# A four-block graph network on one Trainium2 core: the edge weights move to the narrow operand of the matrix-building matmuls, and ScalarE clears every second reused PSUM block

## The chip, the cores and the metric

The kernel runs on one core of one Trainium2 chip. The metric is the device time of one execution in microseconds; lower is better. The core's engines are TensorE (PE in the profile; its weight loads are PEld), VectorE (DVE), ScalarE (ACT), GpSimd (POOL) and SyncE (SP).

## The reference

512 nodes with 512 features each, and 16384 edges sorted by their destination, go through four graph blocks. Each takes `h = relu(layernorm(x))` and adds its result to `x`. Cut to what matters here:

```python
edge_index = stack([src, dst])
x = x + L0(h)   # adj[src,dst] = adj[dst,src] = 1, + I; row-normalised; h@W, then 3 hops of adj @ cur
x = x + L1(h)   # sum_r segment_sum((h[src] @ W_rel[r] + b_rel[r]) * weight * (type == r), dst), / degree; FFN, two layer norms
x = x + L2(h)   # adj[src,dst] = 1, + I, d^-1/2 adj d^-1/2 @ (h @ W)
x = x + L3(h)   # two SAGE layers: mean of h[src] over dst, @ Wl.T, + x @ Wr.T
```

So five 512x512 matrices are wanted from the edge list: for each of the four edge types r the sum of the weights of the edges src to dst, and the count of edges src to dst, from which the unweighted adjacencies come. The function `build_matrices` makes them; `run_blocks` does everything else.

## The kernel before

**The work around the change.** The 16384 edges are 128 chunks of 128 edges, in order of destination; an edge of a chunk sits on a partition. For a chunk PE multiplies one-hot rows: the stationary operand says which of 128 values the low part of `src` has, the moving operand says which destination, edge type and high part of `src` (4 of them) the edge has. The edges of one chunk reach only few destinations, so the moving operand has `WIDE` = 8 destinations from a base on, which is the first destination of the chunk rounded down to an even number (`base`, L321). The columns are then NT x R x WIDE = 4 x 4 x 8 = 128 for the weights and 4 x 8 = 32 for the counts. A float32 weight is split in `V` = 3 bfloat16 parts, and before the change the parts stand in the stationary operand: `wgt_hot` is the low one-hot `lo_hot` times a part. So a chunk is three matmuls of 128 columns (L585) and one of 32 columns (L587), into PSUM at a register offset.

**The PSUM blocks.** Sixteen destinations (`DB`) make a block of 4 x 5 x 22 = 440 float32 columns in one PSUM bank: 16 destinations and 6 of overhang (`TAIL`). There are 32 blocks in 8 banks. PE clears a block with a matmul of zeros of 440 columns (`zero`, L577) before its first chunk, `opens(b)` = 4b - 7. After the last chunk of a block, `closes(b)` = 4b + 7, ACT copies its 16 destinations to `wall` (L279) and its overhang to `tails` (L281), in `keep_block`. DVE adds the overhangs in later (`add_tails`, L416).

**Groups.** 16 chunks (`G`) are a group; there are 8, called group 0 to 7 here. DVE builds the one-hots of a group in a ring of `RING` = 3: `low_hot` and the two `key_hots` by comparison (L370), then the weighted ones by `weigh` (L376). From group 3 on, ACT makes half of the third part (`weigh_some`, L273, 8 instructions a group). DVE waits for PE to have finished the group three before. PE waits for the hots of a group, and reads the 16 PSUM offsets of a group into registers with one TENSOR_LOAD (L550), those of groups 0 to 2 during the projection, of the others ahead of the group. Each matmul at a register offset has an instruction in front that makes its address (printed as ISA). Group 7 is made in two halves, FRONT and BACK.

**Before and behind.** Ahead of the chunks PE runs matmuls of zeros (`spin`), transposes and the projection `h @ W` (L561). Behind them DVE has a fixed list: three `add_tails`, the copy of the early counts (L420), splits and products for block L0 (L434, L426, L429), one more `add_tails`, two splits, then it waits for all chunks, copies the last block (L466), adds its overhang, and signals `built`. With that the copy of the last counts (L515) releases PE (L654) and SyncE's weight loads for the later blocks. Then `run_blocks` begins with the hops (L1132). The order on each engine is written out by hand; semaphores are the only link. A flag computed on the chip (`slow_flag`, L336 to L349) sends all engines down another, much longer path where a chunk's destinations don't fit `WIDE`.

## Time and profile before

| what | value |
|---|---|
| median of 3 runs | 386.3 us (385.6 to 386.51) |
| the profiled execution's own time | 386.04 us |
| its span | 384.1 us, 4220 instructions |
| PE busy | 368.6 us, 96% |
| DVE busy | 181.6 us, 47% |
| ACT busy | 91.5 us, 24% |
| mean granted TensorE clock | 0.991 |

The span is from the first to the last instruction; 1.9 us of the execution's own time lie outside it. Busy shares are averages over stages with different limits. The stretch in which the chunks run is 29 to 69 us of the span, a tenth of it.

### The profile page before, as it was taken

What the parts mean: (1) busy time and instruction counts of PE and PEld (TensorE: products, weight loads), DVE (VectorE), ACT (ScalarE), POOL (GpSimd) and SP (SyncE); (2) the same over time, 40 slices, a digit from 0 to 9 for tenths busy, and PEclk for the clock granted to TensorE, in tenths of its full rate; (3) what the DMA queues carried; (4) which work ended last, traced back from release to release, by engine and by line L of the source; (5) the groups of instructions that cost most, each with busy time, mean ns of one, the idle gap of its engine ahead of it and who ended that gap; (6) DMA issues with size and microseconds to landing.
All of it is one profiled execution on the core that took longest, in us unless ns stands there. A gap on an engine that the chain in (4) does not pass through costs nothing.

```text
span 384.1 us, 4220 instructions
## 1 busy us (share of the span) xinstructions
PE 368.6 (96%) x1554; PEld 205.7 (54%) x1554; DVE 181.6 (47%) x329; ACT 91.5 (24%) x213; POOL 57.9 (15%) x48
## 2 busy tenths in 40 slices
PE   6999787899999999999999999999999999999996
PEld 2448676788444444444444447544455757445642
DVE  5898999968832122236320332004685447212311
ACT  3446986132510000000000102321124270212000
POOL 5000000000589700010001001000211064000000
PEclk9899999899999999999999999999999999999999
DMA  7000000399000000029100018027333000000011
GB/s 249 25 2 2 3 2 2 140 295 363 25 2 0 0 0 0 0 100 355 65 0 0 2 30 189 0 42 124 56 53 59 0 0 2 0 0 0 2 55 55
DMA packets 43812, 22.05 MB, mean 57 GB/s; under 512 B 35536, under 2 KB 36048, under 8 KB 43792
## 3 DMA queue, kind: packets, MB, share of 16 engines
q1 hardware_dynamic: 43264, 20.85, 19.8%
q0 software_dynamic: 240, 0.79, 0.7%
q8 instruction: 14, 0.23, 0.2%
q10 hardware_dynamic: 288, 0.13, 0.1%
q14 instruction: 6, 0.05, 0.0%
HBM read 20.72 MB, written 1.05 MB: 57 GB/s over the span
## 4 chain that ended last, share of the span: by engine, by line
PE 84%; DVE 12%; DMA 1%; ACT 1%; issue 1%; ACTq 0%; DVEq 0%
PE bank L1132 46%; PE bank L1206 14%; PE bank L1325 7%; PE bank L1237 7%; DVE slots L376 4%; PE bank L561 4%; DVE slots L370 3%; PE bank L1120 2%; PE bank L522 1%; DVE wall L416 1%; DMA bias<-in_edge_type 1%; PE bank L585 1%; DVE lo L434 1%; DVE stats L945 1%; PE bank L1148 0%
## 5 line engine op out<-in xcount | busy, mean ns | idle before, releaser
L1132 PE MATMUL bank<-slots,h_t 128*128 128x512 f32 x192 | 83.6, 592 | 0.8 <-ACT h_t L868 0.8
L1132 PEld LDWEIGHTS bank<-slots,h_t 128*128 128x128 f32 x192 | 35.9, 190 | 43.6 <-issue 43.6
L1206 PE MATMUL bank<-slots,wall 128*128 128x512 f32 x128 | 55.7, 593 | 0.0
L1206 PEld LDWEIGHTS bank<-slots,wall 128*128 128x128 f32 x128 | 24.0, 190 | 28.7 <-issue 28.7
L585 PE MATMUL bank<-slots 128*128 128x128 bf16 x384 | 31.8, 219 | 5.7 <-DVE slots L370 3.3
L1013 DVE TENSOR_TENSOR slots<-bank,bias 128x512 f32<-128x512 f32 x16 | 11.1, 692 | 43.9 <-PE bank L1132 43.9
L585 PEld LDWEIGHTS bank<-slots 128*128 128x128 bf16 x384 | 25.0, 97 | 9.0 <-issue 6.5
L1132 PE MATMUL bank<-wall,h_t 128*128 128x512 f32 x64 | 29.0, 594 | 0.5 <-ACT h_t L868 0.5
L1325 PE MATMUL bank<-wall,slots 128*128 128x512 f32 x64 | 28.4, 592 | 0.0
L1132 PE MATMUL bank<-h_t,slots 128*128 128x384 f32 (+2 forms) x96 | 28.0, 451 | 0.0
L1237 PE MATMUL bank<-slots 128*128 128x512 f32 x64 | 27.8, 592 | 0.0
L1132 PE MATMUL bank<-hi,adj 128*128 128x512 f32 x64 | 26.6, 415 | 0.0
L1132 PE MATMUL bank<-lo,adj 128*128 128x512 f32 x64 | 25.8, 403 | 0.0
L376 DVE TENSOR_TENSOR slots<-slots,inv_cnt 128x2048 bf16<-128x2048 bf16 (+1 forms) x26 | 25.5, 1030 | 0.0
L857 ACT ACTIVATE columns<-mean_var,eps 128x1 f32<-128x1 f32 x20 | 5.9, 293 | 74.7 <-DVE mean_var L946 74.6
L370 DVE TENSOR_TENSOR slots<-inv_cnt,both_ways 128x2048 bf16<-128x2048 f16 (+3 forms) x27 | 21.9, 860 | 2.2 <-PE bank L587 1.7
L587 PE MATMUL bank<-slots 128*128 128x32 bf16 x128 | 22.7, 178 | 0.0
L1132 PEld LDWEIGHTS bank<-h_t,slots 128*128 128x128 f32 x96 | 15.7, 191 | 11.6 <-issue 7.7
L1237 PEld LDWEIGHTS bank<-slots 128*128 128x128 f32 x64 | 12.1, 190 | 14.8 <-issue 14.8
L1325 PEld LDWEIGHTS bank<-wall,slots 128*128 128x128 f32 x64 | 12.1, 190 | 14.5 <-issue 14.4
L1030 DVE SCALAR_TENSOR_TENSOR h<-bank,columns,h 128x512 f32<-128x512 f32 x4 | 3.0, 751 | 35.4 <-PE bank L1206 35.4
L818 POOL TENSOR_TENSOR h<-h,bias 128x512 f32<-128x512 f32 x4 | 5.1, 1266 | 95.3 <-PE bank L1120 95.3
(163 smaller groups left out, 452.3 us busy)
## 6 DMA issues: line engine op xcount, KB each, us to landing
slots<-in_L_gnn_W_rel SPq DMA_DIRECT2D x4, 1024.0 KB, 11.1
slots<-in_L_gnn_W_ffn SPq DMA_DIRECT2D x2, 2048.0 KB, 12.8
slots<-in_L_gnn_Wl SPq DMA_DIRECT2D x32, 64.0 KB, 2.4
slots<-in_L_gnn_Wr SPq DMA_DIRECT2D x32, 64.0 KB, 2.4
x<-in_x SPq DMA_DIRECT2D x4, 256.0 KB, 5.4
bias<-in_L_gnn_W SPq DMA_DIRECT2D x1, 1024.0 KB, 7.4
slots<-in_L_gnn_W_self SPq DMA_DIRECT2D x1, 1024.0 KB, 5.8
bias<-in_L_gnn_b_rel SPq DMA_DIRECT2D x4, 256.0 KB, 10.2
```

The source lines that it names most:

```text
L370: return dve.tensor_tensor(to[:, pairs], have, want, ALU.is_equal)
L376: dve.tensor_tensor(wgt_hot[:, s, v, pairs], lo_hot[:, s, pairs], by, ALU.mult).then_inc(hots_ready, 1)
L561: ins = pe.matmul(proj_bank[m], h_t[:, k, m * P:(m + 1) * P], w0[:, k, :], start=(k == 0), stop=(k == KT - 1))
L585: pe.matmul(place[:, :, 0:R, 0:WIDE], wgt_hot[:, s, v, a, :, j], key_hot[:, s, a, :, j], start=False, stop=False, skip_group_check=True)
L587: pe.matmul(place[:, :, R, 0:WIDE], lo_hot[:, s, a, :, j], cnt_hot[:, s, a, :, j], start=False, stop=False, skip_group_check=True).then_in ...
L857: act.activation(std[:, t:t + 1], mean_var[:, t, 1:2], ACT.Sqrt, bias=eps[:]).then_inc(std_ready[n], 1)
L1013: dve.tensor_tensor(msg[r][:, m, :], main[m][:], brel[r], ALU.add).then_inc(msg_out, 1)
L1120: ins = pe.transpose(t_bank[use % 2][:, i * P:(i + 1) * P], b, ident[:])
L1132: ins = pe.matmul(bank, left, right, start=start and i == 0, stop=stop and i == len(pairs) - 1)
L1206: ins = pe.matmul(main[m][:], wall[:, r, s, tile(m)], msg[r][:, s, :], start=(r == 0 and s == 0), stop=(r == R - 1 and s == NT - 1))
L1237: ins = pe.matmul(main[m][:], hid[:, g, tile(m)], wf2[:, g, :], start=(g == 0), stop=(g == GT - 1))
L1325: ins = pe.matmul(sage_bank[m][:], agg_t[layer][:, k, tile(m)], sage(wl, k), start=False, stop=(k == KT - 1))
```

## The change

`WIDE` is 7, and the base is the first destination of the chunk, odd or even. `lo_hot` alone is the stationary operand of every matmul of a chunk. The weights move to the other side: a table `typ_hot` (chunk, type) is made once, times the three parts of the weight (`typ_wgt`, 512 elements a part), and `weigh` multiplies the count one-hots `cnt_hot` (4 x 7 = 28 columns) by it. The weighted hots of part 0 and the count hots are neighbours in `cnt_wgt_hot`, so a chunk is one matmul of 5 x 28 = 140 columns and two of 4 x 28 = 112. ACT makes no hots any more. For every second block from 9 on (9, 11, ... 31) ACT writes the zeros (L285 of the changed kernel), and PE waits for that in place of its own matmul of zeros. The overhang stays 6 and a block 440 columns.

```diff
-WIDE = 8
+WIDE = 7
...
-TAIL = DB - 2 + WIDE - DB
+TAIL = DB - 1 + WIDE - DB
...
-BY_ACT = 8
-ACT_FROM = 3
...
-assert N == D and E % P == 0 and CH == P and NT * R * WIDE == P and NT * OUT_R * COLS <= 512
+assert N == D and E % P == 0 and CH == P and NT * R * WIDE <= P and NT * OUT_R * COLS <= 512
...
-        lo_hot, key_hot = in_slots(BF16, RING, G // 2, P, 2), in_slots(BF16, RING, G // 2, P, 2)
-        cnt_hot, wgt_hot = in_slots(BF16, RING, G // 2, NT * WIDE, 2), in_slots(BF16, RING, V, G // 2, P, 2)
+        lo_hot, cnt_wgt_hot = in_slots(BF16, RING, G // 2, P, 2), in_slots(BF16, RING, G // 2, OUT_R, NT * WIDE, 2)
+        cnt_hot, wgt_hot = cnt_wgt_hot[:, :, :, R], in_slots(BF16, RING, V - 1, G // 2, R, NT * WIDE, 2)
+        typ_hot, typ_wgt = in_slots(BF16, CH // 2, R, 2), in_slots(BF16, V, CH // 2, R, 2)
...
-        lo_set, hots_ready, chunk_done = sem("lo_set"), sem("hots_ready"), sem("chunk_done")
-        block_out = sem("block_out")
+        cnt_set, hots_ready, chunk_done = sem("cnt_set"), sem("hots_ready"), sem("chunk_done")
+        block_out, act_zeroed = sem("block_out"), sem("act_zeroed")
...
+        def zeroed_by_act(b):
+            return b >= 9 and b < NB and b % 2 == 1
...
-            def weigh_some(g):
-                act.wait_ge(lo_set, g + 1)
-                for c in range(BY_ACT):
-                    act.activation(wgt_hot[:, g % RING, V - 1, c // 2, :, c % 2], lo_hot[:, g % RING, c // 2, :, c % 2], ACT.Copy,
-                                   scale=rest[:, 1, g * G + c:g * G + c + 1]).then_inc(act_hots_ready, 1)
...
-                act.wait_ge(parts_ready, 1)
-                kept = 0
-                for g in range(1, CH // G + 1):
-                    if ACT_FROM <= g < CH // G:
-                        weigh_some(g)
-                    while kept < NB - 1 and closes(kept) < g * G:
-                        keep_block(kept)
-                        kept += 1
+                for b in range(NB - 1):
+                    keep_block(b)
+                    if b > 0 and zeroed_by_act(b + 7):
+                        act.wait_ge(block_out, 2 * b)
+                        act.activation(psum[(b + 7) % 8][:, 0:NT * OUT_R * COLS], zeros[:, 0:NT * OUT_R * COLS], ACT.Copy)\
+                            .then_inc(act_zeroed, 1)
...
-            lo, key, cnt_key, apart = (e_f32[:, i, :] for i in range(4))
-            base, bank_of, col_of = (base_i[:, i:i + 1] for i in range(3))
+            lo, cnt_key, kind, apart = (e_f32[:, i, :] for i in range(4))
+            base, bank_of, col_of = e_int[:, 0, 0:1], base_i[:, 1:2], base_i[:, 2:3]
...
-            link(dve.tensor_scalar(base, e_int[:, 0, 0:1], N - 2, None, ALU.bitwise_and))
...
-                 dve.tensor_scalar(col_of, base, DB - 2, None, ALU.bitwise_and),
+                 dve.tensor_scalar(col_of, base, DB - 1, None, ALU.bitwise_and),
...
-            link(dve.scalar_tensor_tensor(key, typ, float(WIDE), apart, ALU.mult, ALU.add))
-            dve.scalar_tensor_tensor(key, high_i, float(R * WIDE) / P, key, ALU.mult, ALU.add).then_inc(keys_ready, 1)
+            dve.tensor_copy(kind, typ).then_inc(keys_ready, 1)
...
-                s = g % RING
-                by = chunks(parts[:, v, :], g, pairs).unsqueeze(2).broadcast_to([P, pairs.stop - pairs.start, P, 2])
-                dve.tensor_tensor(wgt_hot[:, s, v, pairs], lo_hot[:, s, pairs], by, ALU.mult).then_inc(hots_ready, 1)
+                s, count = g % RING, pairs.stop - pairs.start
+                to = cnt_wgt_hot[:, s, pairs, 0:R] if v == 0 else wgt_hot[:, s, v - 1, pairs]
+                at = slice(g * G // 2 + pairs.start, g * G // 2 + pairs.stop)
+                dve.tensor_tensor(to, cnt_hot[:, s, pairs].unsqueeze(2).broadcast_to([P, count, R, NT * WIDE, 2]),
+                                  typ_wgt[:, v, at].unsqueeze(3).broadcast_to([P, count, R, NT * WIDE, 2]),
+                                  ALU.mult).then_inc(hots_ready, 1)
...
-                hot(lo_hot[:, g % RING], 0, g, pairs, P).then_inc(lo_set, 1)
-            def key_hots(g, pairs):
-                hot(key_hot[:, g % RING], 1, g, pairs, P).then_inc(hots_ready, 1)
-                hot(cnt_hot[:, g % RING], 2, g, pairs, NT * WIDE).then_inc(hots_ready, 1)
+                hot(lo_hot[:, g % RING], 0, g, pairs, P).then_inc(hots_ready, 1)
+            def count_hot(g, pairs):
+                hot(cnt_hot[:, g % RING], 1, g, pairs, NT * WIDE).then_inc(cnt_set, 1)
...
+                count_hot(g, WHOLE)
...
-                key_hots(g, WHOLE)
-                dve.wait_ge(lo_set, g + 1)
-                for v in range(V - 1):
+                dve.wait_ge(cnt_set, g + 1)
+                for v in range(V):
...
-                weigh(g, V - 1, BACK if g >= ACT_FROM else WHOLE)
...
+                count_hot(g, FRONT)
+                count_hot(g, BACK)
...
-                key_hots(g, FRONT)
+                dve.wait_ge(cnt_set, g + 2)
+                for v in range(V):
+                    weigh(g, v, FRONT)
...
-                dve.wait_ge(lo_set, g + 1)
-                for v in range(V - 1):
-                    weigh(g, v, FRONT)
-                key_hots(g, BACK)
-                dve.wait_ge(lo_set, g + 2)
...
-                low_hot(0, WHOLE)
+                types = chunks(keys_t[:, 2, :], 0, slice(0, CH // 2)).unsqueeze(2).broadcast_to([P, CH // 2, R, 2])
+                kinds = pair_iota[:, 0:R, :].unsqueeze(1).broadcast_to([P, CH // 2, R, 2])
+                dve.tensor_tensor(typ_hot, types, kinds, ALU.is_equal).then_inc(typ_set, 1)
+                count_hot(0, WHOLE)
...
-                key_hots(0, WHOLE)
+                dve.wait_ge(typ_set, 1)
+                for v in range(V):
+                    by = chunks(parts[:, v, :], 0, slice(0, CH // 2)).unsqueeze(2).broadcast_to([P, CH // 2, R, 2])
+                    dve.tensor_tensor(typ_wgt[:, v], typ_hot, by, ALU.mult).then_inc(typ_set, 1)
...
-                dve.wait_ge(lo_set, 1)
-                weigh(0, 0, WHOLE)
+                low_hot(0, WHOLE)
...
-                for v in range(1, V):
+                dve.wait_ge(cnt_set, 1)
+                dve.wait_ge(typ_set, 1 + V)
+                for v in range(V):
...
+                if zeroed_by_act(b):
+                    pe.wait_ge(act_zeroed, (b - 7) // 2)
+                    return
                 if b >= 8:
...
-                for v in range(V):
-                    pe.matmul(place[:, :, 0:R, 0:WIDE], wgt_hot[:, s, v, a, :, j], key_hot[:, s, a, :, j],
-                              start=False, stop=False, skip_group_check=True)
-                pe.matmul(place[:, :, R, 0:WIDE], lo_hot[:, s, a, :, j], cnt_hot[:, s, a, :, j],
-                          start=False, stop=False, skip_group_check=True).then_inc(chunk_done, 1)
+                low = lo_hot[:, s, a, :, j]
+                pe.matmul(place[:, :, :, 0:WIDE].rearrange("p h r d -> p r h d"), low, cnt_wgt_hot[:, s, a, :, :, j],
+                          start=False, stop=False, skip_group_check=True)
+                for v in range(V - 1):
+                    ins = pe.matmul(place[:, :, 0:R, 0:WIDE].rearrange("p h r d -> p r h d"), low, wgt_hot[:, s, v, a, :, :, j],
+                                    start=False, stop=False, skip_group_check=True)
+                ins.then_inc(chunk_done, 1)
...
-                            pe.wait_ge(hots_ready, (V + 2) * (g + 1) - (0 if g < CH // G - 1 else 1))
-                            if g >= ACT_FROM:
-                                pe.wait_ge(act_hots_ready, BY_ACT * (g - ACT_FROM + 1))
-                        elif c == CH - G + BY_ACT:
-                            pe.wait_ge(hots_ready, (V + 2) * (g + 1) + V + 1)
+                            pe.wait_ge(hots_ready, (V + 1) * (g + 1))
+                        elif c == CH - G // 2:
+                            pe.wait_ge(hots_ready, (V + 1) * (g + 2))
```

On PE, the rows of group 3 from its load of offsets on; `slots` are the one-hots, `both_ways` the zeros. Before:

```order
L550 TENSOR_LOAD both_ways
L585 ISA
L585 MATMUL bank<-slots 128x4x4x8 x3
L587 ISA
L587 MATMUL bank<-slots 128x4x8
L577 MATMUL bank<-both_ways 128x440
L585 ISA
L585 MATMUL bank<-slots 128x4x4x8 x3
L587 ISA
L587 MATMUL bank<-slots 128x4x8
L585 ISA
```

And of the changed kernel:

```order
L549 TENSOR_LOAD both_ways
L587 ISA
L587 MATMUL bank<-slots 128x5x4x7
L590 MATMUL bank<-slots 128x4x4x7 x2
L579 MATMUL bank<-both_ways 128x440
L587 ISA
L587 MATMUL bank<-slots 128x5x4x7
L590 MATMUL bank<-slots 128x4x4x7 x2
L587 ISA
L587 MATMUL bank<-slots 128x5x4x7
L590 MATMUL bank<-slots 128x4x4x7 x2
L587 ISA
```

A chunk has three matmuls for four and one address instruction for two; its runs in PSUM are 7 columns long for 8.

On DVE, the rows of group 4, from its wait for PE on; L370 compares, L376 multiplies, L416 adds overhangs. Before:

```order
L370 TENSOR_TENSOR slots<-inv_cnt,both_ways 128x2048 [waits chunk_done]
L370 TENSOR_TENSOR slots<-inv_cnt,both_ways 128x2048
L370 TENSOR_TENSOR slots<-inv_cnt,both_ways 128x512
L376 TENSOR_TENSOR slots<-slots,inv_cnt 128x2048 [waits lo_set]
L376 TENSOR_TENSOR slots<-slots,inv_cnt 128x2048
L376 TENSOR_TENSOR slots<-slots,inv_cnt 128x1024
L416 TENSOR_TENSOR wall<-wall,bias 128x20x4x6 [waits block_out]
```

And of the changed kernel (L362 compares, L369 multiplies, L408 adds overhangs):

```order
L362 TENSOR_TENSOR slots<-inv_cnt,both_ways 128x8x56 [waits chunk_done]
L362 TENSOR_TENSOR slots<-inv_cnt,both_ways 128x2048
L369 TENSOR_TENSOR slots<-slots 128x8x224 [waits cnt_set]
L369 TENSOR_TENSOR slots<-slots 128x1792 x2
L408 TENSOR_TENSOR wall<-wall,bias 128x20x4x6 [waits block_out]
L362 TENSOR_TENSOR slots<-inv_cnt,both_ways 128x8x56 [waits chunk_done]
```

A group has one comparison of 2048, one of 448 and three products of 1792 elements, for two of 2048, one of 512, and products of 2048, 2048 and 1024; nothing of it is left to ACT.

On ACT, rows in the middle of the chunks; `wall` and `bias` receive a kept block. Before:

```order
L281 ACTIVATE bias<-bank 128x4x5x6
L273 ACTIVATE slots<-slots 128x128 [waits lo_set]
L273 ACTIVATE slots<-slots 128x128 x7
L279 ACTIVATE wall<-bank 128x4x5x16 [waits chunk_done]
L281 ACTIVATE bias<-bank 128x4x5x6
L279 ACTIVATE wall<-bank 128x4x5x16 [waits chunk_done]
L281 ACTIVATE bias<-bank 128x4x5x6
```

And of the changed kernel:

```order
L275 ACTIVATE wall<-bank 128x4x5x16 [waits chunk_done]
L277 ACTIVATE bias<-bank 128x4x5x6
L285 ACTIVATE bank<-both_ways 128x440 [waits block_out]
L275 ACTIVATE wall<-bank 128x4x5x16 [waits chunk_done]
L277 ACTIVATE bias<-bank 128x4x5x6
L275 ACTIVATE wall<-bank 128x4x5x16 [waits chunk_done]
L277 ACTIVATE bias<-bank 128x4x5x6
L285 ACTIVATE bank<-both_ways 128x440 [waits block_out]
```

The eight scaled copies of a group are gone, and behind every second kept block stands a write of 440 zeros to the bank that was kept one block earlier.

## Rows read from the trace of the kernel before

**Rows 1.** Page of the profile, part 4: shares of the chain by line

```profile
...
PE bank L1132 46%; PE bank L1206 14%; PE bank L1325 7%; PE bank L1237 7%; DVE slots L376 4%; PE bank L561 4%; DVE slots L370 3%; PE bank L1120 2%; PE bank L522 1%; DVE wall L416 1%; DMA bias<-in_edge_type 1%; PE bank L585 1%; DVE lo L434 1%
...
```

**Rows 2.** Chain that ended last, in order: start us, us, engine, output, line

```profile
...
5.01 0.29 DVE bias L332
...
33.49 2.70 DVE slots L370 x3
...
39.05 2.60 DVE slots L370 x3
41.66 2.87 DVE slots L376 x3
...
57.20 2.01 DVE slots L370 x4
...
63.02 1.72 DVE wall L416 x3
...
70.73 0.41 DVE wall L466
...
72.28 0.55 PE bank L654 x3
...
```

**Rows 3.** Groups from 29 to 73 us, shapes apart: busy us, mean ns

```profile
...
L585 PE MATMUL bank<-slots 128*128 128x128 bf16 x384 | 31.8, 219 | 5.7 <-DVE slots L370 3.3 <-ACT slots L273 1.2 <-issue 1.2
...
L587 PE MATMUL bank<-slots 128*128 128x32 bf16 x128 | 22.7, 178 | 0.0
L279 ACT ACTIVATE wall<-bank 128x320 f32<-128x320 f32 x31 | 13.6, 440 | 9.6 <-PE bank L587 9.5
L376 DVE TENSOR_TENSOR slots<-slots,inv_cnt 128x2048 bf16<-128x2048 bf16 x11 | 12.9, 1216 | 0.0
...
L281 ACT ACTIVATE bias<-bank 128x120 f32<-128x120 f32 x31 | 8.5, 275 | 0.0
L376 DVE TENSOR_TENSOR slots<-slots,inv_cnt 128x1024 bf16<-128x1024 bf16 x9 | 5.9, 681 | 0.0
...
L370 DVE TENSOR_TENSOR slots<-inv_cnt,both_ways 128x512 bf16<-128x512 f16 x4 | 1.7, 416 | 0.0
...
```

**Rows 4.** Timeline of PE: start us, us, line, operation, count

```profile
...
33.68 0.34 PE L585 MATMUL bank<-slots 128*128 128x128 bf16 x3
...
33.88 0.33 PE L585 MATMUL bank<-slots 128*128 128x128 bf16 x3
...
34.48 0.35 PE L577 MATMUL bank<-both_ways 128*128 128x440 bf16 x1
34.66 0.34 PE L585 MATMUL bank<-slots 128*128 128x128 bf16 x3
...
41.11 0.18 PE L587 MATMUL bank<-slots 128*128 128x32 bf16 x1
42.27 0.35 PE L585 MATMUL bank<-slots 128*128 128x128 bf16 x3 [0.98 <-DVE slots L370]
...
67.50 0.34 PE L585 MATMUL bank<-slots 128*128 128x128 bf16 x3
...
67.75 0.34 PE L585 MATMUL bank<-slots 128*128 128x128 bf16 x3
...
68.49 0.18 PE L587 MATMUL bank<-slots 128*128 128x32 bf16 x1
...
```

**Rows 5.** Offset loads of L550 on PE's queue: duration ns min/median/max

```profile
...
L550 PEldq TENSOR_LOAD <-both_ways x8: 1102/1105/1292, 13.7 to 62.9; - x8
...
```

**Rows 6.** Windows: us, busy by engine, PEclk (granted clock), DMA, GB/s

```profile
...
69.00:74.00 5.00, 3.76 (x25) 3.48 (x25) 4.44 (x11) 0.31 (x2) 0.00 (x0) 0.94 0.14 49
74.00:78.00 4.00, 4.00 (x13) 3.22 (x12) 3.43 (x11) 0.00 (x0) 0.00 (x0) 0.65 1.03 372
...
```

**Rows 7.** Timeline of ACT with a backlog

```profile
...
40.23 0.42 ACT L279 ACTIVATE wall<-bank 128x320 f32<-128x320 f32 x1
...
40.70 0.44 ACT L279 ACTIVATE wall<-bank 128x320 f32<-128x320 f32 x1
...
```

More of the change, by code:

```diff
@@ L162, in build_matrices @@
         const_set, ident_ready, const_ready = sem("const_set"), sem("ident_ready"), sem("const_ready")
-        zeros_set, act_hots_ready = sem("zeros_set"), sem("act_hots_ready")
+        zeros_set, typ_set = sem("zeros_set"), sem("typ_set")
         eye_set, iota_ready = sem("eye_set"), sem("iota_ready")
@@ L179, in build_matrices @@
         chunked = "(c e) -> c e"
-        WHOLE, FRONT, BACK = slice(0, G // 2), slice(0, BY_ACT // 2), slice(BY_ACT // 2, G // 2)
+        WHOLE, FRONT, BACK = slice(0, G // 2), slice(0, G // 4), slice(G // 4, G // 2)
         most = slice(0, N - P)
@@ L550, in offsets @@
                 return nc.values_load_multi_w_load_instructions(
-                    off_row[0:1, g * G:(g + 1) * G], [PE], min_val=0, max_val=7 * N + DB - 2,
+                    off_row[0:1, g * G:(g + 1) * G], [PE], min_val=0, max_val=7 * N + DB - 1,
                     skip_runtime_bounds_check_because="masked to that on the chip")[1]
```

## The prediction

> **What bounds the kernel now.** I read the shares of the chain first: nearly all of the span is PE in the blocks behind the matrices (the hops, L1132, and L1206, L1237, L1325), which the change doesn't touch [rows 1]. In the stretch of the chunks the chain lies on DVE. It enters DVE at 33.49, when PE has finished group 0 and a place in the ring is free, and stays there: group 4 is 2.60 of comparisons (39.05) and 2.87 of products (41.66), group 7 begins at 57.20, the hots are done at 63.02, the fixed list behind them runs to the copy of the last block at 70.73, and PE takes over at 72.28 [rows 2]. So hots made faster pull everything behind them forward, until something else is later than the list.
>
> PE is that something, and close. In group 1 a chunk follows the last one after 0.20 (33.68, 33.88), and a matmul of zeros takes 0.18 (34.48, 34.66). Groups 0 to 2 end at 41.11, and the next chunk starts only at 42.27; the last chunk ends at about 68.6 [rows 4]. The gap is no lack of hots: group 3's were done at 39.05 [rows 2]. It is the TENSOR_LOAD of the offsets, 1.1 us each time [rows 5], which starts when the queue is empty. So PE's groups 3 to 7 take (68.49 - 41.11) / 5 = 5.48 each [rows 4]: 16 x 0.196 + 4 x 0.19 = 3.9 of matmuls (0.196 is the pitch of chunks to three digits) and 1.58 around the load. DVE needs all chunks at 70.73, so PE has 2.1 us in hand.
>
> **DVE, part by part.** Instructions overlap by 0.08: two comparisons of 2048 and one of 512 have means of 1216 (the product's mean, the form costs the same) and 416, in sum 2.85, and take 2.60 [rows 2, 3]. The slope is (1216 - 681) / 1024 = 0.52 ns an element [rows 3]. Then 1792 elements take 1.00 net, 448 take 0.30, 2048 take 1.14, 1024 take 0.60, 896 take 0.53 and 224 take 0.19. A group after: 0.30 + 1.14 + 3 x 1.00 = 4.45, for 2.60 + 2.87 = 5.47 before. That is 1.02 less in each of groups 3 to 6: 4.1. Group 7 took 63.02 - 57.20 = 5.82 and will take 2 x 0.19 + 2 x 0.60 + 6 x 0.53 = 4.77: 1.05. The `add_tails` between groups stay as they are.
>
> I take the new products at the same slope. They read both inputs with a step of 0 in some dimension, but innermost are pairs of neighbouring 16-bit values as before. If they fell to one element per step, 0.52 ns more for each of 1792 elements, a group would take 2.8 more. The other end is no cost below the slope: nothing in the rows runs faster.
>
> The first three groups and the table (four instructions of 512, 0.33 each, 1.3 in sum) lie ahead of 33.49, where DVE waited 1.66 for PE; they cost nothing, since the shorter groups 0 to 2 also give back more than that. If PE came earlier, this cover would still hold by some 4 us.
>
> **The start.** DVE enters the chain by group 0 of PE. Two things bring that forward. Ahead of the transposes one copy stands for two products of 0.29 (L331, L332) [rows 2]; that is up to 0.33, and 0.15 if the fixed zeros matmuls behind it swallow half; I take 0.2. And PE's group 0 is shorter. A column at 2.4 GHz is 0.42 ns, and the 440 columns of zeros take that, 0.18 [rows 4]. A chunk before has 3 x 128 + 32 = 416 columns, 0.173, and takes 0.196: 0.006 over for each of four matmuls. A chunk after has 140 + 2 x 112 = 364 columns, 0.152, and three times 0.006: 0.170. Group 0 is 16 x 0.026 = 0.4 shorter. Together 0.6.
>
> Sum: 4.1 + 1.05 + 0.6 = 5.75, call it 5.8.
>
> **Does PE stay ahead?** It starts at 29.2. Groups 0 to 2: 48 chunks and 9 zeros (blocks 2 to 8, 10, 12; the others are ACT's). Groups 3 to 7: 80 chunks, 9 zeros, five loads at 1.58. With c for a chunk, PE ends at 29.2 + 18 x 0.19 + 7.9 + 128c = 40.5 + 128c. For c = 0.170 that is 62.3, and DVE asks at 70.7 - 5.8 = 64.9: 2.6 us of room. It is filled at c = 0.191. The whole gain is gone at c = (70.7 - 40.5) / 128 = 0.236. Where PE's sequencer sets the pace, with no zeros in between, chunks came every 0.25 (67.50, 67.75) [rows 4]; with one address instruction and three matmuls for two and four this is 0.125 (by the address instructions) to 0.19 (by the matmuls), and I take it as no slower than the array. If it stayed 0.25 in groups 3 to 7, a group would take 16 x 0.25 + 1.58 = 5.6, PE would end near 67, and some 2 of the 5.8 would go.
>
> **ACT.** It loses eight copies a group and gains two writes of 440 zeros. L279 and L281 give (440 - 275) / 200 = 0.83 ns a column, so 440 columns take 0.54 [rows 3]. With a backlog a kept block takes 0.47 (40.23, 40.70) [rows 7]. A group is then 4 x 0.47 + 2 x 0.54 = 3.0 for 4.45 of DVE: idle. In groups 0 to 2 eight chunks take PE 8 x 0.170 + 0.19 = 1.55 and ACT 2 x 0.47 + 0.54 = 1.48: just enough, with 14 chunks between the block kept before the write and the chunk that needs it. Behind the waiting PE instruction all chunks are queued; a lag of ACT would cost PE at most the 0.54 each time, from its 2.6 of room.
>
> **The branch.** The 128 chunks of the reference's inputs reach at most 5 destinations beyond their first, and 7 allow 6, so the long path isn't taken.
>
> **The hops.** At 73 to 77 the granted clock fell to the lower of its two levels (0.94 and 0.65 in the two windows, 3.4 us at 1.2 GHz in sum), right behind PE's pause before L654; it cost 1.7 [rows 6]. After the change PE is done with the chunks at 62.3, turns the early counts, and then has nothing until 72.3 - 5.8 = 66.5: a longer pause, so a low stretch at the hops is at least as likely. It may be as long (0), longer, at most double (+1.7), or fall where PE is idle (-1.7). I take 0 and keep both ends. A low clock among the chunks, where PE's matmuls would fill 3.1 of the 5.0 us of a DVE group for 3.9 of 5.5, I hold unlikely: the gap of a load was 1.16 [rows 4] and grows no longer.
>
> **Forecast.** 386.04 - 5.8 = 380.2 for the profiled execution, whose own time is 0.3 below the median of the runs; so 380.5 as the median. Its own range is 378 to 382.
>
> **Rivals.** *PSUM runs of odd length.* The new columns lie in runs of 7 from any column on; before, runs of 8 from an even one. No row of before shows such a write. For it: the base was rounded down to an even number at the price of an eighth column, and contiguous zeros and runs of 8 have the same 0.42 ns a column, so runs that start even are the only thing known to be fast. Against it: nothing shown. The lower bound is no cost, c = 0.170. If a run of 7 costs as one of 8, a chunk is 160 + 2 x 128 = 416 columns again, 0.191: PE ends at 64.9, just in time. If columns are written in pairs of the stream, and pairs that straddle two even places go twice, two runs of 7 take 11 steps for 7: 364 x 11 / 7 = 572 columns, c = 0.256, PE ends at 73.3, the list waits from 70.7 on, 2.6 slower: 389. If every column takes double, c = 0.31, PE ends at 80.2, 9.5 slower: 396. This decides from c = 0.236 on. The Trainium skill, PSUM — Partial Sum Buffer, section Specifications (TRN2), has 8-byte lines (two float32) and says that any access that is not contiguous slows matmuls significantly. For runs of 8 the trace disagrees, whose chunk takes 0.196 for 416 columns; by its rule applied to the new runs the time would be the 389 to 396 just given. The rival has 0.14.
>
> *PE takes over in part.* c between 0.19 and 0.23, by the writes or the sequencer, or zeros that come late from ACT: 381 to 385.5, at 383. 0.15.
>
> *Nothing gained.* c near 0.236, or the DVE gain eaten by a second low stretch and a late PE together: 386. 0.05.
>
> *DVE's products lose the pairs, or the clock falls among the chunks.* Five groups x 2.8 - 5.8 = 8 slower, 394; or c doubled, 396. The innermost pairs and the gap speak against them. 0.04.
>
> **How the numbers follow.** The forecast has 0.62, the rivals 0.14, 0.15, 0.05 and 0.04. A measurement of this kernel can tell 0.3%, 1.2 us, from no change. Faster: 0.62 + 0.15 = 0.77; same 0.05; slower 0.18. The range that leaves out 0.18 above and a few hundredths below is 377.8 to 385.8: it takes in PE's part take-over and both ends of the hops' clock.
>
> **What would show it.** DVE: 21 products of 1792 with a mean of 1.08 us, groups of 4.45, and 0.57 more with `add_tails`. PE: chunks 0.170 apart in group 1, up to 0.19 later, the five gaps at 1.1 to 1.3 as before, last chunk at 62 to 65. ACT: 12 writes of 0.54, none waited for. PE resumes with the last counts at 66.5 for 72.28. Wrong: chunks of group 1 more than 0.19 apart (the PSUM runs), DVE idle before it copies the last block, products near 2.0, or a granted clock below 1 between 30 and 60.

## The result, and the profile after it

The changed kernel takes 381.63 us (median of 4 runs, 380.98 to 381.81), the kernel before 386.4 in the same comparison (385.6 to 387.34, 4 runs): ratio 0.9873, 95% interval 0.9847 to 0.9898. That is 4.8 us faster for a forecast of 5.8. The profiled executions differ by 4.54 in their own time and by 4.77 in span, because 2.2 us lie outside the span after the change, for 1.9 before.

| | before | after |
|---|---|---|
| profiled execution: own time, span | 386.04, 384.09 | 381.5, 379.32 |
| mean granted clock of PE | 0.991 | 0.987 |
| first chunk on PE | 29.38 | 28.83 |
| DVE released by group 0 | 33.49 | 32.80 |
| hots done | 63.02 | 57.16 |
| fixed list, hots done to last counts on PE | 9.26 | 9.28 |
| last chunk on PE starts | 68.3 | 58.7 |
| PE resumes with the last counts | 72.28 | 66.44 |
| from there to the end | 311.81 | 312.88 |

The chain of waits of the changed kernel answers to [rows 2]: start us, us, engine, output, line.

```profile
...
32.80 1.53 DVE slots L362 x2
34.33 3.00 DVE slots L369 x3
...
47.36 1.44 DVE slots L362 x2
48.80 3.01 DVE slots L369 x3
...
52.38 0.97 DVE slots L362 x3
...
57.16 1.72 DVE wall L408 x3
...
65.95 0.44 DVE cnt_r L514
66.44 0.90 PE bank L656 x3
...
68.62 19.67 PE bank L1134 x78
...
```

DVE enters the chain at 32.80 and keeps it, as before. A group is 47.36 to 52.38: 1.44 of comparisons, 3.01 of products and 0.57 of `add_tails`, so 4.45 of hots for 5.47. From 32.80 to 57.16 the hots take 24.36, for 29.53 from 33.49 to 63.02: 5.17 less. At 66.44 PE takes over. The 78 matmuls of the hops then take 19.67, for 19.57 in the kernel before, whose chain has them at:

```profile
...
73.51 19.57 PE bank L1132 x78
...
```

Most of what is lost behind 66.44 lies ahead of these 78: from PE's resuming to their start 2.18 pass (66.44, 68.62), for 1.23 before (72.28, 73.51).

The groups from 29 to 73 us, shapes apart, answer to [rows 3]: busy us, mean ns, idle time before and its releaser.

```profile
...
L587 PE MATMUL bank<-slots 128*128 128x140 bf16 x128 | 25.8, 242 | 1.3 <-DVE slots L369 1.3
...
L369 DVE TENSOR_TENSOR slots<-slots 128x1792 bf16<-128x1792 bf16 x12 | 12.4, 1090 | 0.0
...
L285 ACT ACTIVATE bank<-both_ways 128x440 f32<-128x440 bf16 x12 | 6.6, 551 | 0.0
...
L362 DVE TENSOR_TENSOR slots<-inv_cnt,both_ways 128x448 bf16<-128x448 f16 x4 | 1.6, 392 | 3.9 <-PE bank L590 3.9
...
```

The product of 1792 elements has a mean of 1090 ns: the slope of 0.52 ns an element holds, the pairs are kept. DVE waited 3.9 us for PE ahead of 32.80, so the table and the reordered first groups were covered. ACT's twelve writes of zeros take 0.55 each. PE's only wait in the chunks is 1.3, and it is for hots.

The timeline of PE, which answers to [rows 4]: start us, us, line, operation, count, idle time before and its releaser.

```profile
...
30.32 0.24 PE L587 MATMUL bank<-slots 128*128 128x140 bf16 x1
...
30.50 0.24 PE L587 MATMUL bank<-slots 128*128 128x140 bf16 x1
...
31.07 0.24 PE L587 MATMUL bank<-slots 128*128 128x140 bf16 x1
...
31.27 0.24 PE L587 MATMUL bank<-slots 128*128 128x140 bf16 x1
...
39.52 0.24 PE L587 MATMUL bank<-slots 128*128 128x140 bf16 x1
...
39.83 0.24 PE L587 MATMUL bank<-slots 128*128 128x140 bf16 x1
...
58.75 0.28 PE L590 MATMUL bank<-slots 128*128 128x112 bf16 x2
60.01 0.41 PE L650 MATMUL bank<-cnt_r,ident_r 128*128 128x384 f32 x1 [0.98 <-DVE cnt_r L412]
...
61.51 0.56 PE L644 MATMUL bank<-ident_r,cnt_r 128*128 128x128 f32 x4
66.44 0.90 PE L656 MATMUL bank<-cnt_r,ident_r 128*128 128x128 f32 x3 [4.37 <-DVE cnt_r L514]
...
```

Chunks come 0.18 or 0.20 apart, where the forecast had 0.170 throughout. Across the offset load at group 3, 0.31 passes from chunk to chunk (39.52, 39.83). Before, it was 1.33 (to 42.27 of [rows 4]) from this row of its timeline:

```profile
...
40.94 0.33 PE L585 MATMUL bank<-slots 128*128 128x128 bf16 x3
...
```

PE is done with the chunks at 59.0 and with the early counts at 62.1, and then stands for 4.37 until 66.44. Ahead of L654 that pause was 1.16 before.

Windows that answer to [rows 6]: us, busy time of each engine, granted clock, DMA share, GB/s.

```profile
...
64.00:69.00 5.00, 2.56 (x10) 2.37 (x11) 4.29 (x12) 0.00 (x0) 0.00 (x0) 0.65 0.35 106
69.00:73.00 4.00, 4.00 (x12) 3.15 (x11) 2.73 (x9) 0.00 (x0) 0.00 (x0) 0.58 1.06 365
...
```

The granted clock is at the lower level (1.2 GHz) from about 65.5, when PE stands, to 72.3: some 6.8 us, for 3.4 before [rows 6].

### The profile page after: what moved, and what is told of

It reads as the page before. It is cut to its first block, busy times and chain, and to the rows that moved or that the text cites. A ratio compares the mean times of both kernels' runs of the same rounds, so it can differ in the third digit from the quotient of the medians.

```text
span 379.3 us, 3773 instructions
## 1 busy us (share of the span) xinstructions
PE 364.6 (96%) x1414; PEld 203.1 (54%) x1414; DVE 172.8 (46%) x323; ACT 85.6 (23%) x185; POOL 57.9 (15%) x48
## 3 DMA queue, kind: packets, MB, share of 16 engines
HBM read 20.72 MB, written 1.05 MB: 57 GB/s over the span
## 4 chain that ended last, share of the span: by engine, by line
PE 86%; DVE 11%; DMA 1%; ACT 1%; issue 1%; ACTq 0%; DVEq 0%
PE bank L1134 47%; PE bank L1208 15%; PE bank L1327 7%; PE bank L1239 7%; DVE slots L369 4%; PE bank L560 4%; PE bank L1122 2%; DVE slots L362 2%; PE bank L521 1%; DVE wall L408 1%; DMA bias<-in_edge_type 1%; DVE lo L426 1%; DVE stats L947 1%; PE bank L590 0%; PE bank L543 0%
## 5 line engine op out<-in xcount | busy, mean ns | idle before, releaser
L587 PE MATMUL bank<-slots 128*128 128x140 bf16 x128 | 25.8, 242 | 1.3 <-DVE slots L369 1.3
L590 PE MATMUL bank<-slots 128*128 128x112 bf16 x256 | 26.9, 228 | 0.0
L1134 PE MATMUL bank<-hi,adj 128*128 128x512 f32 x64 | 26.7, 417 | 0.0
L369 DVE TENSOR_TENSOR slots<-slots 128x1792 bf16<-128x1792 bf16 (+1 forms) x27 | 25.0, 986 | 0.0
L590 PEld LDWEIGHTS bank<-slots 128*128 128x128 bf16 x256 | 22.5, 103 | 1.7
L1134 PEld LDWEIGHTS bank<-wall,h_t 128*128 128x128 f32 x64 | 11.7, 190 | 13.4 <-issue 13.4
```

Source lines behind the costliest of these rows:

```text
L369: dve.tensor_tensor(to, cnt_hot[:, s, pairs].unsqueeze(2).broadcast_to([P, count, R, NT * WIDE, 2]), typ_wgt[:, v, at].unsqueeze(3).broadc ...
L587: pe.matmul(place[:, :, :, 0:WIDE].rearrange("p h r d -> p r h d"), low, cnt_wgt_hot[:, s, a, :, :, j], start=False, stop=False, skip_grou ...
L590: ins = pe.matmul(place[:, :, 0:R, 0:WIDE].rearrange("p h r d -> p r h d"), low, wgt_hot[:, s, v, a, :, :, j], start=False, stop=False, sk ...
L1134: ins = pe.matmul(bank, left, right, start=start and i == 0, stop=stop and i == len(pairs) - 1)
```

## The experiments

"Stretch" below is the time from the first chunk to PE's resuming with the last counts: 42.90 before (72.28 - 29.38), 37.61 after (66.44 - 28.83). Numbers "from the profile" are of one execution.

### PE kept busy ahead of the last counts

`after_spins` is the changed kernel with this; `before_spins` is the kernel before with 5 for 18.

```diff
                 add_turned(t, NT - 1, True)
+            pe.wait_ge(block_out, 2 * (NB - 3))
+            for _ in range(18):
+                pe.matmul(psum[4], zeros[:, 0:P], zeros, start=True, stop=True)
             pe.wait_ge(late_kept, 1)
```

> The changed kernel with 18 matmuls of zeros on PE in the pause between its early counts and its wait for the last ones. Theory (the low clock at the hops costs 3 us and comes from the pause of 4.4 us): the granted clock stays at 2.4 GHz from 61 to 80, L656 still starts at 66.4, and the time falls by 2 to 3 us, to about 379. Rival (what is missing of the forecast 5.8 is lost in the later blocks or in transfers, and the low stretch comes whatever PE does before): 381.6, or more if the zeros hold PE up.

Measured: 380.57 (379.09 to 381.04) beside 386.29, ratio 0.9845 (0.9814 to 0.9876). The timeline of PE:

```profile
...
8.71 4.43 PE L521 MATMUL bank<-both_ways 128*128 128x512 bf16 x10
12.94 0.88 PE L543 MATMUL bank<-ident,h 128*128 128x128 f32 x4
...
63.04 0.56 PE L644 MATMUL bank<-ident_r,cnt_r 128*128 128x128 f32 x4
63.43 4.06 PE L656 MATMUL bank<-both_ways 128*128 128x512 bf16 x18
67.97 0.55 PE L659 MATMUL bank<-cnt_r,ident_r 128*128 128x128 f32 x3 [0.47 <-DVE cnt_r L514]
...
```

The last three rows: the pause shrinks to 0.47, and the 18 zeros stand in it. (The first two are spoken of at the end.) The granted clock stays at 1.00, and from PE's resuming to the end it is 378.24 - 67.97 = 310.27, for 312.88: 2.6 less. The stretch is 37.60. So the low clock costs 2.6 us in the profile of after; against the 1.6 that before paid already, it is the 1.07 that was lost. The median moved by 1.1, for 2 to 3 expected; in the profile the first chunk starts 1.54 later than in after (30.37), and the other executions have no profile.

The 1.07 belongs to this pair of profiles. Seven profiles of the changed kernel and its variants have the same pause ahead of the last counts, 4.37 or 4.38. From resuming to the end they take 311.88 (`pe_clears`), 311.94 (`solid_runs`), 312.00 (`wide7_even`), 312.46 (`wide8_even`), 312.88 (after), 313.08 (`changed_again`) and 313.32 (`start_fill`), for 310.2 without a low stretch. So the same pause costs from 1.6 to 3.1, and before, behind a pause of 1.16, paid 1.6 too. What differs is how much of the low stretch lies behind PE's resuming: 3.4 us before, 3.7 in `pe_clears`, 5.9 in after, 6.8 in `start_fill`. A little under half of that is lost each time.

> The kernel before with 5 matmuls of zeros in the same place, where its pause was 1.2 us. Theory: its low stretch of 3.4 us at the hops goes too, 1.7 us less, 384.7; the distance to the changed kernel with zeros is then the full 5.8 of the hots and the start. Rival (the stretch has other causes than the pause): 386.4 and the same low stretch.

Measured: 385.85 (384.68 to 387.25), ratio 0.9985 (0.9965 to 1.0004), for 384.7 expected. The distance to `after_spins` is 5.3 in the medians, for 5.8 expected. In the profile resume to end is 310.24 for 311.81, 1.57 less, as expected; but the first chunk starts at 30.46 for 29.38, and the median gained only 0.4. The executions of before with a mean clock of 0.999 or 1.0, 6 of 48 in the comparisons of this study, took 385.8 to 386.2, the five of `before_spins` with 1.0 took 385.6 to 386.3: the kernel before isn't caught at the hops in all of its executions. What share of the missing 1.2 this explains stays open.

### The zeros back on PE, and the zeros on ACT alone

`pe_clears` is the changed kernel with

```diff
-            return b >= 9 and b < NB and b % 2 == 1
+            return False
```

> The changed kernel, but PE clears all blocks again and ACT none. Theory (DVE is the bound and PE has some 6 us in hand): PE's last chunk comes 1 to 3 us later, L465 starts at the same 64.8, the time is 381.6 within 0.5. Rival (ACT's clears are what brought PE forward, and the time with it): 383 or more.

Measured: 382.9 (382.07 to 384.02), ratio 0.9918 (0.9888 to 0.9948). The stretch is 37.61 (31.07 to 68.68), to the hundredth that of after. PE's last chunk comes 0.45 later from the first one, for 1 to 3 expected, and nobody waits for it. The profile's later end is its first chunk, 2.24 later, less 1.0 at the hops. So ACT's clears are worth nothing in the profiled stretch. The median alone wouldn't say so: 382.9 lies 0.8 to 1.3 above the two medians of the changed kernel (381.63, and 382.06 below), outside the 0.5 expected and near the rival's 383. The intervals of the ratios overlap (0.9888 to 0.9948, and 0.9844 to 0.9896 for `changed_again`); that starts as late as the profiled one explain it is likely and not shown.

`before_act_clears` puts the same writes into the kernel before:

```diff
                         keep_block(kept)
+                        if kept > 0 and zeroed_by_act(kept + 7):
+                            act.wait_ge(block_out, 2 * kept)
+                            act.activation(psum[(kept + 7) % 8][...], zeros[...], ACT.Copy).then_inc(act_zeroed, 1)
...
+                if zeroed_by_act(b):
+                    pe.wait_ge(act_zeroed, (b - 7) // 2)
+                    return
```

> The kernel before with the second half of the change alone: ACT clears blocks 9, 11, ... 31. Theory (DVE is the bound there too): DVE's hots end at 63.0 as before, PE earlier by up to 2 us, time 386.4 within 0.5. Rival (PE's chunks were a bound of their own): 384 to 385.

Measured: 386.07 (384.53 to 388.51), ratio 1.0 (0.9975 to 1.0024); stretch 42.92, hots done at 63.08. This part alone is worth nothing either.

### The base even, with runs of 7 and of 8

Both round the base down to an even destination, as before; `wide8_even` also sets `WIDE = 8`, `TAIL = DB - 2 + WIDE - DB`. `wide7_even` leaves 7.

```diff
+            link(dve.tensor_scalar(base, e_int[:, 0, 0:1], N - 2, None, ALU.bitwise_and))
...
-                 dve.tensor_scalar(col_of, base, DB - 1, None, ALU.bitwise_and),
+                 dve.tensor_scalar(col_of, base, DB - 2, None, ALU.bitwise_and),
```

> The changed kernel with 8 destinations a chunk from an even base, so products of 2048 elements and matmuls of 160 and 128 columns. Theory for DVE (0.52 ns an element): groups of 4.88 for 4.45, so 4 x 0.43 + 0.45 = 2.2 us slower at the copy of the last block, and one more dependent instruction of 0.2 at the start that is hidden: 383.8. Theory for PE (a run of 7 costs as a run of 8): chunks 0.19 to 0.20 apart, as in the changed kernel. Rival for PE (the pitch goes by columns, with something fixed of 0.013 a matmul): chunks 0.213 apart.

Measured: 383.94 (383.1 to 385.62), ratio 0.9935 (0.9909 to 0.9962). The stretch is 39.74 (31.13 to 70.87), 2.13 more, for 2.2 expected: products of 2048 for 1792 on DVE. The chunks on PE, from its timeline:

```profile
...
32.63 0.23 PE L588 MATMUL bank<-slots 128*128 128x160 bf16 x1
...
32.81 0.24 PE L588 MATMUL bank<-slots 128*128 128x160 bf16 x1
...
33.00 0.23 PE L588 MATMUL bank<-slots 128*128 128x160 bf16 x1
...
```

A chunk of 416 columns follows after 0.187 on the mean, 0.45 ns a column. That is a little less than the theory's 0.19 to 0.20, and the rival's 0.213 is out.

> The changed kernel with 7 destinations from a base rounded down to an even number (the reference's chunks still fit). Only the parity of the places in PSUM differs, and one small DVE instruction at the start. Theory (a run of 7 touches as many pairs from an even as from an odd place): chunks 0.19 apart as before, time 381.6 within 1. Rival (places that start odd cost more than those that start even): chunks below 0.18 apart, the time still 381.6 because PE has room.

Measured: 381.9 (379.94 to 382.39), ratio 0.9884 (0.9841 to 0.9928), stretch 37.51. The mean pitch of the chunks is 0.183, between the two expectations: less than the 0.190 of after, so odd starts do cost, and more than the rival's figure, so they aren't all of it. In the changed kernel itself, with the chunks of its timeline sorted by their base in the inputs (those with a load or zeros behind them left out), the 52 with an even base take 0.184 on the mean and the 50 with an odd one 0.201. In `wide7_even`, where all places are even, the same two sets take 0.184 and 0.183, so it is the place and not the chunk. A run of 7 from an even place (0.184) costs nearly what a run of 8 does (0.187).

### Runs made solid

Here the products go to neighbouring columns, so the matrices are not the reference's; only the pace is read.

```diff
-                place = flat[:, bass.ds(at, NT * OUT_R * COLS)].rearrange("p (h r d) -> p h r d", h=NT, r=OUT_R)
+                solid = flat[:, bass.ds(at, NT * OUT_R * COLS)]
...
-                pe.matmul(place[:, :, :, 0:WIDE].rearrange("p h r d -> p r h d"), low, ...
+                pe.matmul(solid[:, 0:OUT_R * NT * WIDE], low, ...
...
-                    ins = pe.matmul(place[:, :, 0:R, 0:WIDE].rearrange("p h r d -> p r h d"), low, ...
+                    ins = pe.matmul(solid[:, 0:R * NT * WIDE], low, ...
```

> The changed kernel, but the 140 and 112 columns of a chunk go to neighbouring places in PSUM in place of runs of 7, so the matrices come out wrong; only the pitch is read. Theory (the pitch of 0.19 comes from runs of odd length): 0.170 apart in the first groups. Rival (it comes from the loads of weights or from a fixed cost of a matmul): 0.19 as before.

One run: 380.24, span 378.0. The timeline of PE:

```profile
...
30.93 0.23 PE L587 MATMUL bank<-slots 128*128 128x140 bf16 x1
...
31.09 0.23 PE L587 MATMUL bank<-slots 128*128 128x140 bf16 x1
...
31.26 0.22 PE L587 MATMUL bank<-slots 128*128 128x140 bf16 x1
...
31.42 0.23 PE L587 MATMUL bank<-slots 128*128 128x140 bf16 x1
...
```

A chunk follows after 0.165. The stretch is 37.23, 0.38 less, and group 0 accounts for all of it: 16 x (0.190 - 0.165) = 0.40. So the runs cost 0.025 a chunk, and only the sixteen of group 0 reach the end.

### A second address instruction for each chunk

Two of the three matmuls write one type further, so the matrices are not the reference's; their address differs from the first one's, and PE's sequencer has to work it out.

```diff
-                    ins = pe.matmul(place[:, :, 0:R, 0:WIDE].rearrange("p h r d -> p r h d"), low, ...
+                    ins = pe.matmul(place[:, :, 1:OUT_R, 0:WIDE].rearrange("p h r d -> p r h d"), low, ...
```

> The changed kernel, but the second and third matmul of a chunk write one edge type further (wrong matrices; only times are read), which needs a second address instruction a chunk. Theory (the address instruction is most of the sequencer's 0.245 a chunk, and with one of them the sequencer runs ahead and hides the load of offsets): chunks 0.22 to 0.25 apart late in a group, and gaps at the five loads of 1.1 to 1.3 again for 0.33; PE's last chunk at 62 to 64; the time unchanged within 1. Rival (the gap vanished for another reason, fewer matmuls in the queue): gaps stay at 0.33.

One run: 383.81, span 381.6. In groups 0 to 2 the pitch is 0.196, later 0.225, and 1.41 passes at each of the five loads. In the changed kernel it is 0.27 to 0.34 at four of them; the one at group 6 coincides with PE's wait of 1.3 for hots. The load's own duration hasn't changed. The address instructions on PE's queue, count: ns min/median/max. Of this kernel, of the changed one and of before (the rows of one line each):

```profile
...
L590 PEldq FUSED_REGOPS  x128: 46/46/51, 27.3 to 68.7; - x128
...
```

```profile
...
L587 PEldq FUSED_REGOPS  x128: 37/37/42, 24.8 to 58.1; - x128
...
```

```profile
...
L585 PEldq FUSED_REGOPS  x128: 42/42/42, 25.4 to 68.2; - x128
...
```

So with one address instruction a chunk PE's sequencer runs ahead far enough to take most of the 1.1 us load beside the matmuls; with two it is exposed. The start of the load for group 3 shows it: 38.6 in the changed kernel, 0.9 ahead of the last chunk of group 2 (39.52), but 40.9 before, where that chunk starts at 40.94, and 42.3 here, where it starts at 42.14. The theory's "most of the sequencer's 0.245" isn't borne out: an address instruction has 37 to 46 ns by these rows, so two are 0.09. I had expected the last chunk at 62 to 64 and the end unmoved within 1 us; the last chunk starts at 68.7, and the stretch grew by 2.5, to 40.15. DVE stands for blocks that ACT keeps as PE finishes them, and at the end the last counts start on PE only when its early counts are through (71.39, DVE was done at 71.04). The timeline of DVE:

```profile
...
62.47 0.66 DVE L408 TENSOR_TENSOR wall<-wall,bias 128x480 f32<-128x480 f32 x1 [1.76 <-ACT bias L277]
...
67.67 0.66 DVE L408 TENSOR_TENSOR wall<-wall,bias 128x480 f32<-128x480 f32 x1 [0.31 <-ACT bias L277]
...
```

The 6 us that PE has in hand in the changed kernel (59.0 for 64.80, where the last block is copied) were used up: here is where PE would take over.

### The changed kernel again, and PE kept busy at the start and at the hops

The profiles' first chunk lay between 28.8 and 31.2 in kernels that don't differ ahead of it, so I ran the changed kernel again and moved five of its ten zeros matmuls (`spin(10)`, L546) ahead of PE's first wait for the plan (`start_fill`). `both_fills` has the 18 of `after_spins` too.

```diff
+            spin(5)
             pe.wait_ge(plan_in, 3)
...
-            spin(10)
+            spin(5)
```

> The changed kernel itself once more, to be compared on one chip with the three below, since its profile and those of its variants begin the chunks at 28.8 to 31.2 us with the same code ahead of them. Theory (the clock at the start falls for 3.4 or for 6.8 us from one execution to the next, whatever the kernel): 381 to 383, spread over 2 us or more, and chunks that begin anywhere from 28.8 to 31.2. Rival (the start belongs to the kernel): 381.6 within 0.5, chunks from 28.8 on.

> The changed kernel with 5 of its 10 fixed matmuls of zeros moved ahead of PE's wait for the plan, where PE pauses 1.5 to 2.5 us. Theory (that pause lets the clock fall): no low stretch from 8 to 15, chunks begin at 27 to 29, and 1 to 2 us less than the changed kernel on this chip; the hops keep their low stretch of 6.8. Rival (the start waits for the plan and the loads, not for the clock): same time.

> The changed kernel with the 5 moved matmuls and with 18 more in the pause ahead of the last counts. Theory: the two gains add, clock at 2.4 GHz from the start to the end; 2.6 us less at the hops and 1 to 2 at the start: 377.5 to 379. Rival: no more than after_spins, 380.5.

Measured beside 386.15 for before: `changed_again` 382.06 (379.88 to 382.7), ratio 0.987 (0.9844 to 0.9896), spread over 2.8 and with its first chunk at 29.83, as the theory had it; `start_fill` 380.11 (379.18 to 380.22), 0.9827 (0.9804 to 0.985), 1.95 less; `both_fills` 377.18 (376.71 to 377.39), 0.9758 (0.9737 to 0.9779), 2.9 less again and just below the expected range. Windows of `changed_again`, then of `both_fills`, columns as above:

```profile
...
5.00:15.00 10.00, 7.33 (x31) 3.86 (x32) 7.68 (x33) 3.69 (x8) 0.94 (x2) 0.83 0.51 179
...
60.00:75.00 15.00, 9.64 (x40) 8.26 (x40) 11.94 (x28) 0.67 (x3) 0.00 (x0) 0.66 0.45 152
...
```

```profile
...
5.00:15.00 10.00, 9.67 (x41) 5.04 (x41) 8.62 (x35) 4.57 (x10) 0.95 (x2) 1.00 0.52 181
...
60.00:75.00 15.00, 14.47 (x67) 10.55 (x67) 14.13 (x31) 2.65 (x4) 0.00 (x0) 1.00 0.65 183
...
```

The first profile has two low stretches, 3.4 us in the first window, 10.2 in the last; the second has none. `start_fill` has the first gone (1.00) and the second still there (0.66), 10.2 us long for 6.8 expected. The first chunk starts at 26.69 in `both_fills` for 28.83 in after, 78 hop matmuls take 17.96 for 19.67, and the stretch is 37.61 once more. So the span of after, 379.32, less 2.14 at the start and 2.6 at the hops is the 374.5 measured. In the medians, 382.06 to 377.18, it is 4.9.

The gain at the start is not all clock, a rival that the expectations left out. PE has no pause from the transpose of the plan (L534, L535 here) to the first chunk, and the ten zeros stand in that path; five of them now don't. The path takes 19.17 in `start_fill` (7.74 to 26.91), for 21.45 in after. Of these 2.3, an estimate of 5 x 0.214 = 1.07 would be gained at the full clock too, by the pace of the other five (below). The rest, 1.2, is left for the clock; no run separates the two.

### Runs of 6 on top

```diff
-WIDE = 7
+WIDE = 6
...
-TAIL = DB - 1 + WIDE - DB
+TAIL = 6
```

> both_fills with 6 destinations a chunk, which is what the widest chunk of the reference's inputs needs; the overhang stays at 6. Theory (DVE's hots are still the bound, 0.52 ns an element): groups of 4.02 for 4.45, 2.1 us less than both_fills, and chunks of 312 columns below 0.18. Rival (with DVE faster PE or ACT takes over): less than 1 us.

Measured: 374.25 (374.12 to 375.89), ratio 0.9694 (0.9671 to 0.9718), 2.9 less than `both_fills`, where I had expected 2.1. The chain of waits:

```profile
...
34.45 1.40 DVE slots L362 x2
35.85 2.61 DVE slots L369 x3
...
61.80 0.55 PE bank L660 x3
63.03 17.98 PE bank L1138 x78
...
```

A group of hots is 34.45 to 38.45, 4.00 for 4.44 in `both_fills`. In all, the hots give 2.18 (24.36 to 22.18), and group 0 on PE 0.57 (3.98 to 3.41), mostly because the chunk's pitch falls, to 0.157 in groups 0 to 2 and 0.160 over all: 2.75 together. My 2.1 left group 0 out. Sorted by base as above, the 52 chunks with an even base take 0.146 on the mean and the 49 with an odd one 0.175. This kernel still computes the reference for these inputs, whose widest chunk reaches 5 destinations beyond its first; one that reached 6 would take the long path.

## Why the prediction was right, and where not

**What bounds it, and the slope of DVE: right.** The hots were forecast to give 4.1 + 1.05 = 5.15 and gave 5.17; the product 1.08, measured 1.09; the fixed list moved as one piece (9.26, 9.28). `wide8_even` and `six_both` scale the same product up and down and move the stretch by +2.13 and -2.75, which is DVE's slope and, in the second, group 0.

**ACT, the clears and the branch: right.** 0.54 forecast, 0.551 measured, none waited for, and both experiments on the clears leave the stretch as it was. The 1.55 of PE and 1.48 of ACT for a pair of blocks was never put to the test, since PE didn't wait.

**"I take 0" for the hops: the term that was mis-sized.** It measured +1.07 in the two profiles. The direction was in the text, "a longer pause, so a low stretch at the hops is at least as likely", and the upper end, +1.7, held it. By the forecast PE would have been done with the chunks at 62.3 and with the early counts some 2 us later, which leaves a pause of about 2. It was 4.37 long, since PE was earlier (see the loads, below). `after_spins` shows that the low stretch comes from PE standing there: no pause, no low stretch, 2.6 back. It doesn't show that the longer pause made the stretch dearer: three profiles with the same 4.37 lose 1.6 to 1.8, hardly more than before's 1.6, and for them 0 was right to about 0.2. With 1.07 in the sum the forecast would have been 381.6, near the median of 381.63; how much of the median is the hops isn't known.

**The start, "together 0.6": the size right by luck, the parts not.** Group 0 gave 0.14 for 0.4, because a chunk takes 0.190 for 0.170. The first chunk came 0.55 earlier for 0.2. The rows of PE's wait for the plan, before and after, have all of it, 0.53:

```profile
...
7.91 0.27 PE L535 MATMUL bank<-ident,bias 128*1 128x128 f32 x1 [1.84 <-DVE bias L342]
...
```

```profile
...
7.38 0.28 PE L534 MATMUL bank<-ident,bias 128*1 128x128 f32 x1 [1.53 <-DVE bias L334]
...
```

From there to the first chunk it is 21.47 and 21.45. But it can't be put down to the copy at L324: in profiles with the same instructions as after up to there, this wait ends at 7.4 to 8.4, and behind it 21.45 to 22.8 pass, by how long PE's pace is low. So their first chunks start between 28.8 and 31.2.

**The chunk's pitch: wrong by 0.020, which cost 0.26 in group 0 and nothing behind it.** The rival "PSUM runs of odd length" exists as a mechanism and is small. Solid 0.165, runs of 7 from even bases 0.184, from odd ones 0.201, with the columns and instructions the same: 11 to 22% over solid, far from the 0.236 at which the gain would be gone. Runs that pay 11 steps for 7 columns would have given 0.256, and are excluded. The Trainium skill, PSUM — Partial Sum Buffer, section Specifications (TRN2), says that any access that is not contiguous slows matmuls significantly. For runs of 8 from an even place the trace disagrees (0.187 for 416 columns, 0.45 ns each, as the solid 364 in 0.165), and for runs of 7 it agrees in kind, at those 11 to 22%.

**PE's loads, "1.58 around the load": wrong in the kernel's favour.** The gap is 0.27 to 0.34 where no wait for hots covers it. I had carried it over from before as a property of a load that "starts when the queue is empty". It belongs to a sequencer that two address instructions a chunk keep from running ahead: with the second one back it is 1.41. That is why PE ended at 59.0 for 62.3 forecast, in spite of the longer pitch, and why the rival "PE takes over in part", worked out with c between 0.19 and 0.23, didn't come although c was 0.19. `two_addresses` shows it in one execution, and that a pitch of 0.225 with the old gaps takes 2.5 of the gain.

**Open.** Why `before_spins` gains 1.57 in its profile behind L654 and only 0.4 in the median. Why the low stretch at the hops begins where it does, and so costs 1.6 in one profile and 3.1 in another. And which share of the 4.8 is owed to where the starts and the low stretches fell: the medians of the changed kernel, 381.63 and 382.06, differ by less than its own runs do (379.9 to 382.7).

## What to carry to other kernels

Where a DVE list bounds a stretch, the elements taken out of it times the measured slope are the gain, here to a few hundredths (5.17 for 5.15), as long as the other engine's margin is worked out with them. When an upstream engine gets faster, ask what the engine behind it does in the time it wins: here PE stood for 4.37, its clock fell, and the next dense stretch lost 1.6 to 3.1, for 1.6 before. Eighteen matmuls of zeros in that pause and five moved into another were worth as much again as the change (4.9), of which about 1 is only that five stand no longer in PE's path. A gap at a load may depend on the instructions queued around it, here the address instructions, so count those before carrying the gap over. And where a pause is followed by a low clock, one profile of each kernel doesn't price it: compare several.

## What the runs showed of the hardware that I had not expected

- **The granted clock shows falls, and not the slow beginning.** In `after_spins` the windows from 5 to 15 us have a granted clock of 1.00, but the trace has no clock record there (its first is at about 13.5), and ten zeros matmuls of 512 columns pass from 8.71 to 12.94 (the rows shown with that kernel): 0.423 each, the pace of 1.2 GHz. In `both_fills` five pass from 8.05 to 9.12, 0.214 each, the pace of 2.4 GHz. The timeline of PE in `both_fills`:

```profile
...
6.11 1.36 PE L521 MATMUL bank<-both_ways 128*128 128x512 bf16 x5
...
8.05 1.24 PE L521 MATMUL bank<-both_ways 128*128 128x512 bf16 x5
9.12 0.60 PE L544 MATMUL bank<-ident,h 128*128 128x128 f32 x4
...
```

- That makes three kinds of start. A low pace up to 13 us or so without a record: first chunk at 30.4 (`after_spins`) or 29.95 (`wide7_even`). Full early and 3.4 us low from about 8 on: 28.8 to 28.9 (after, `solid_runs`), or 29.8 behind a pause of 2.44 (`changed_again`). 6.8 us low: 31.1 to 31.2 (`pe_clears`, `wide8_even`, `two_addresses`, each behind a pause of about 2.5). With five matmuls in the pause, and five fewer behind it: 26.7 to 26.9.
- **The pause doesn't fix how long the low stretch behind it is.** Behind 4.37 us of standing ahead of the last counts it was 6.8 us in after and 10.2 in `changed_again` and `start_fill`; behind 1.16 it was 3.4 in before. What a low stretch costs goes by how much of it lies behind PE's resuming: 3.7 us in `pe_clears` cost 1.6, 5.9 in after 2.6, 6.8 in `start_fill` 3.1, all behind the same pause.
- **Odd places in PSUM cost** 0.017 a chunk of 364 columns in runs of 7 (0.184, 0.201) and 0.028 a chunk of 312 in runs of 6 (0.146, 0.175). A run of 8 from an even place costs nothing that shows: 0.45 ns a column, as in solid runs. A run of 7 from an even place saves next to nothing against one of 8 (0.184, 0.187).
- **An address that comes from a register costs PE's sequencer** 37 to 46 ns each; two a chunk of three or four matmuls were enough to expose a load of 1.1 us (gaps of 1.33 and 1.41), and with one a gap of about 0.3 is left.
